# Layer 0's attention matrix as the stationary operand of the mixing product

## The reference

```python
energy = einsum('bnc,bcm->bnm', x_q, x_k)        # x_q = (w_qk y)^T, x_k = w_qk x
attention = softmax(energy, axis=-1)
attention = attention / (1e-07 + attention.sum(axis=1, keepdims=True))
x_r = einsum('bcn,bnm->bcm', x_v, attention)     # x_v = w_v x + b_v
x_r = relu(einsum('oc,bcn->bon', w_t, x - x_r) + b_t)
x1 = x + x_r
```

## Time and profile before

| | before |
|---|---|
| median of 3 runs | 177.25 us (177.08 to 178.58) |
| span of the profiled execution | 174.3 us |
| PE busy | 149.8 us, 86% |
| DVE busy | 113.1 us, 65% |
| ACT busy | 99.7 us, 57% |
| POOL busy | 88.6 us, 51% |
| the chain that ended last, PE's share | 58% |

### The profile page before, as it was taken

How to read it: one execution, slowest core, us unless ns; L and a number is a source line. 1 busy time by engine, 2 the same in 40 slices (tenths; PEclk the granted TensorE clock), 3 DMA queues, 4 the chain that set the end, 5 groups by cost and what they waited for, 6 DMA issues and landing times.

```text
span 174.3 us, 3459 instructions
## 1 busy us (share of the span) xinstructions
PE 149.8 (86%) x1228; PEld 115.7 (66%) x1228; DVE 113.1 (65%) x249; ACT 99.7 (57%) x242; POOL 88.6 (51%) x143
## 2 busy tenths in 40 slices
PE   7699999999968795779972983865999999999994
PEld 6475677787843372545852852653787999888993
DVE  1445444997885227898999999998476630377310
ACT  2017877779867856557566865955875525255000
POOL 8905608478988850686145695698542544000000
PEclk9999999999999999579997598798799999999999
DMA  2998320201201100000000000000000001000101
GB/s 73 308 223 276 63 64 0 64 0 60 66 11 50 60 0 0 4 2 0 4 2 0 4 4 0 0 4 0 0 0 4 0 30 64 30 0 2 34 30 60
DMA packets 6722, 6.94 MB, mean 40 GB/s; under 512 B 956, under 2 KB 6098, under 8 KB 6706
## 3 DMA queue, kind: packets, MB, share of 16 engines
q1 hardware_dynamic: 5808, 5.85, 10.4%
q0 software_dynamic: 224, 0.33, 1.8%
q10 hardware_dynamic: 674, 0.56, 1.0%
HBM read 5.68 MB, written 1.05 MB: 39 GB/s over the span
## 4 chain that ended last, share of the span: by engine, by line
PE 58%; DVE 15%; POOL 13%; issue 7%; ACT 3%; DMA 2%; POOLq 0%; DVEq 0%
PE psum L779 53%; DVE probs L732 3%; DVE smax L740 3%; POOL us L338 3%; DMA vec_rows<-in_L_xattn_b_t_dram 2%; DVE psums L615 2%; PE psum L1007 2%; DVE probs L747 2%; POOL wpj_lo L314 2%; POOL wfc_lo L314 1%; POOL hidT_lo L366 1%; POOL rstd L302 1%; POOL probs L375 1%; POOL rows L319 1%; DVE xn L631 1%
## 5 line engine op out<-in xcount | busy, mean ns | idle before, releaser
L338 POOL TENSOR_SCALAR us<-uext,rinv 128x128 f32<-128x128 f32 x32 | 12.4, 399 | 15.8 <-DVE rinv L594 15.2
L375 POOL TENSOR_TENSOR probs<-probs,pinv 128x512 f32<-128x512 f32 x16 | 16.5, 1055 | 7.0 <-DVE pinv L620 7.0
L779 PE MATMUL psum<-wpj_hi,ff_hi 128*128 128x256 f32 x64 | 18.3, 286 | 0.0
L779 PE MATMUL psum<-wpj_hi,ff_lo 128*128 128x256 f32 x64 | 17.9, 280 | 0.0
L779 PE MATMUL psum<-wpj_lo,ff_hi 128*128 128x256 f32 x64 | 17.9, 280 | 0.0
L392 ACT ACTIVATE ys<-psum,vec 128x512 f32<-128x512 f32 x16 | 11.0, 687 | 10.5 <-PE psum L779 10.3
L673 DVE TENSOR_REDUCE nmax<-psum 128x2 f32<-128x512 f32 x16 | 10.3, 685 | 9.4 <-PE psum L779 9.4
L779 PE MATMUL psum<-att,us 128*128 128x256 f32 x64 | 15.2, 381 | 0.7 <-POOL us L338 0.7
L779 PE MATMUL psum<-hidT_hi,wfc_hi 128*128 128x512 f32 x32 | 13.8, 432 | 2.0 <-POOL hidT_lo L366 2.0
L437 ACT ACTIVATE att<-psum,nmax 128x256 f32<-128x256 f32 x32 | 14.7, 471 | 0.3 <-DVE nmax L673 0.2
L534 ACT ACTIVATE probs<-probs 128x512 f32<-128x512 f32 x16 | 9.9, 629 | 8.7 <-DVE probs L747 8.4
(11 more groups left out here) (111 smaller groups left out, 396.8 us busy)
## 6 DMA issues: line engine op xcount, KB each, us to landing
wstage<-in_L_xattn_fc_w_dram SPq DMA_DIRECT2D x4, 256.0 KB, 5.8
wstage<-in_L_xattn_proj_w_dram SPq DMA_DIRECT2D x4, 256.0 KB, 2.7
out_dram<-rows SPq DMA_DIRECT2D x8, 128.0 KB, 1.7
ys<-in_ctx_dram SPq DMA_DIRECT2D x1, 512.0 KB, 6.1
rows<-in_x_dram SPq DMA_DIRECT2D x1, 512.0 KB, 8.4
ys<-in_ctx_dram ACTq DMA_DIRECT2D x1, 384.0 KB, 5.2
rows<-in_x_dram SPq DMA_DIRECT2D x1, 384.0 KB, 5.9
wk<-in_L_xattn_k_w_dram SPq DMA_DIRECT2D x1, 256.0 KB, 6.2
```

The costliest lines, as they stand in the source:

```text
L338: pool.tensor_scalar(us[:, n % 2, e, j, :], uext[:, n % 2, j, e * C:e * C + P], rinv[:, n % 2, e, j:j + 1], 1.0, ALU.mult, ALU.mult).then_ ...
L375: pool.tensor_tensor(half, half, pinv[:, n % 2, k].unsqueeze(2).broadcast_to([P, H // 2, C]), ALU.mult).then_inc(S["probs_ready"], 1)
L779: return pe.matmul(dst, lhsT, rhs, start=start, stop=stop)
```

## The change

- The mixing product is transposed: `att` is the stationary operand (128 columns of it at a time) and `us` moves, now only 65 columns: 64 of scaled u, and the inverse row sum, which makes the column sum. A pair takes 8 products instead of 4. The result has positions on partitions, and one column sum for each.
- u and w_t x come from one pass: stationary `rows` (64 x 128, one image), moving `wtvt` = [(w_t w_v)^T, w_t^T], 128 columns. Four products on 64 rows of the array in place of two on 128. The separate product `wtx` goes. Results of the two images lie in banks 3 and 4. DVE takes them out at once with both biases (`evict_uw`), into four buffers `uw`.
- All four results of a mixing lie in one bank, 5, for every pair; it is no longer doubled.
- DVE inverts the column sums (`colsum`, `csinv`, 128 x 4 each) and makes `rin` in four operations of 64 columns. PE turns `rin` back by two transposes (`turn_rin`), and one DVE operation takes relu and residual (`residual`). ACT's Ln, Exp and relu, DVE's `mix_normed` and POOL's residual go.
- ACT, not DVE, copies `gx` out, between the exponentials of image 0 and of image 1.
- b_v and b_t come by DMAs into the layout in which they are used; their transpose on PE goes.

The core of the diff:

```diff
+        PROJ0, ENERGY, UW, BACK, MIX, TURN, FILL = 0, 1, 3, 4, 5, 6, 7
         MLP_BANKS = [4, 5, 4, 5]
-        SETUP_WT, SETUP_GRAM, SETUP_WTV, SETUP_VEC0, SETUP_WTBV, SETUP_VEC = 6, 5, 3, 4, 4, 6
+        SETUP_WT, SETUP_GRAM, SETUP_WTV, SETUP_WTBV, SETUP_VEC = 6, 5, 3, 5, 6
...
+        uw_ps = psum[:, UW:UW + 2, D:2 * D].rearrange("p e (j b c) -> p e j b c", j=2, b=2)
+        mix_ps = psum[:, MIX, 0:4 * (C + 2)].rearrange("p (k c) -> p k c", k=4)
...
-            load_vec(pool, 0, "b_v", L0_BV, vec0_loaded)
-            load_vec(pool, 0, "b_t", L0_BT, vec0_loaded)
+            pool.dma_start(bv_col[:], A["L0_xattn_b_v"].rearrange("(c o) -> c o", o=1)).then_inc(bv_loaded, 16)
+            pool.dma_start(brow[:, 1, :], A["L0_xattn_b_t"].rearrange("(o c) -> o c", o=1)
+                           .broadcast_to([P, C])).then_inc(bt_loaded, 16)
...
-            def residual(n):
-
-                wait(pool, "relu_out", n + 1)
-                pool.tensor_tensor(rows[:, n, :], rows[:, n, :], rout[:], ALU.add).then_inc(S["x1_ready"], 1)
...
-                            pool.tensor_scalar(us[:, n % 2, e, j, :], uext[:, n % 2, j, e * C:e * C + P],
-                                               rinv[:, n % 2, e, j:j + 1], 1.0, ALU.mult,
+                            pool.tensor_scalar(us[:, n % 2, e, j, 0:C], uw[:, n % 4, e, j, 0, :],
+                                               us[:, n % 2, e, j, C:C + 1], 1.0, ALU.mult,
                                                ALU.mult).then_inc(S["scaled_u"], 1)
-                if 0 <= t - 2 < N - 1:
-                    residual(t - 2)
...
                         gelu(act, 0, u)
 
-            def relu(n):
-                wait(act, "relu_in", n + 1)
-                wait(act, "x1_ready", n)
-                if n == 0:
-                    act.wait_ge(vec0_ready, 1)
-                act.activation(rout[:], rin[:, n % 2, :], ACT.Relu, bias=col(L0_BT)).then_inc(S["relu_out"], 1)
+            def gx_copy(n):
+                wait(act, "gx_made", n + 1)
+                wait(act, "energy_made", 2 * (n - 1))
+                act.copy(gx[:, n % 2, :], halfbank(PROJ0, 0)).then_inc(S["gx_ready"], 1)
...
                 if 0 <= t < N:
                     energy_exp(t, 0)
+                if 0 <= t + 1 < N:
+                    gx_copy(t + 1)
                 if 0 <= t < N:
                     energy_exp(t, 1)
-                if 0 <= t - 2 < N - 1:
...
                     fill(u)
-                n = t - 1
-                if 0 <= n < N:
-
-                    wait(act, "mixed", 2 * n + 2)
-                    for e in range(2):
-                        act.activation(csln[e * C:(e + 1) * C, :],
-                                       psum[(1 - e) * C:(2 - e) * C, MIX + n % 2, e * D:(e + 1) * D], ACT.Ln,
-                                       bias=COLSUM_EPS).then_inc(S["colsum_ln"], 1)
-                    wait(act, "colsum_ln", 2 * n + 2)
-                    wait(act, "mix_normed", 2 * n)
...
-                if t == N:
-                    relu(N - 1)
...
             def rowsum_inv(n, e):
                 wait(dve, "energy_exp", 2 * (2 * n + e + 1))
-                wait(dve, "scaled_u", 4 * (n - 1))
-                dve.reciprocal(rinv[:, n % 2, e, :], rsum[:, n % 2, e, :]).then_inc(S["rowsum_inv"], 1)
-
-            def mix_normed(n):
-
+                wait(dve, "mixed", 2 * (n - 2) + e + 1)
+                dve.reciprocal(us[:, n % 2, e, :, C], rsum[:, n % 2, e, :]).then_inc(S["rowsum_inv"], 1)
+
+            def evict_uw(n):
+                wait(dve, "uw_made", n + 1)
+                if n == 0:
+                    dve.wait_ge(wtbv_made, 1)
+                    dve.tensor_copy(brow[:, 0, :], psum[:, SETUP_WTBV, 0:C]).then_inc(wtbv_ready, 1)
+                    dve.wait_ge(wtbv_ready, 1)
+                    dve.wait_ge(bt_loaded, 16)
+                dve.tensor_tensor(uw[:, n % 4].rearrange("p e j b c -> p e j (b c)"),
+                                  uw_ps.rearrange("p e j b c -> p e j (b c)"),
+                                  brow[:].rearrange("p b c -> p (b c)").unsqueeze(1).unsqueeze(1)
+                                  .broadcast_to([P, 2, 2, P]), ALU.add).then_inc(S["uw_ready"], 1)
+
+            def relu_in(n):
+
+                wait(dve, "mixed", 2 * n + 2)
+                dve.tensor_scalar(colsum[:], mix_ps[:, :, C], -1.0, -COLSUM_EPS, ALU.mult,
+                                  ALU.add).then_inc(S["colsum_eps"], 1)
+                wait(dve, "colsum_eps", n + 1)
+                dve.reciprocal(csinv[:], colsum[:]).then_inc(S["colsum_inv"], 1)
                 wait(dve, "colsum_inv", n + 1)
-                for e in range(2):
-                    dve.tensor_tensor(mixn[e * C:(e + 1) * C, :],
-                                      psum[e * C:(e + 1) * C, MIX + n % 2, e * D:(e + 1) * D],
-                                      csinv[e * C:(e + 1) * C, :], ALU.mult).then_inc(S["mix_normed"], 1)
-
-            def relu_in(n):
-
-                wait(dve, "mix_normed", 2 * n + 2)
-                wait(dve, "wtx_made", n + 1)
-                wait(dve, "relu_out", n - 1)
-                dve.tensor_tensor(rin[:, n % 2, :], halfbank(WTX, 0), mixn[:],
-                                  ALU.subtract).then_inc(S["relu_in"], 1)
+                wait(dve, "rin_turned", n - 1)
+                for i in range(2):
+                    for e in range(2):
+                        k = 2 * i + e
+                        dve.scalar_tensor_tensor(rin[:, n % 2, i, e * C:(e + 1) * C], mix_ps[:, k, 0:C],
+                                                 csinv[:, k:k + 1], uw[:, n % 4, e, i, 1, :], ALU.mult,
+                                                 ALU.add).then_inc(S["rin_ready"], 1)
+
+            def residual(n):
+                wait(dve, "rin_turned", n + 1)
+                dve.scalar_tensor_tensor(rows[:, n, :], halfbank(BACK, 0), 0.0, rows[:, n, :], ALU.max,
+                                         ALU.add).then_inc(S["x1_ready"], 1)
 
...
+                if 0 <= t - 3 < N - 2:
+                    residual(t - 3)
...
-                n = t + 1
-                if 0 <= n < N:
-                    wait(dve, "proj_made", n + 1)
-                    dve.tensor_copy(gx[:, n % 2, :], halfbank(PROJ0, 0)).then_inc(S["proj_ready"], 1)
-                    wait(dve, "scaled_u", 4 * (n - 1))
-                    if n == 0:
-                        dve.wait_ge(wtbv_made, 1)
-                        dve.tensor_copy(wtbv[:], psum[:, SETUP_WTBV, 0:P]).then_inc(wtbv_ready, 1)
-                        dve.wait_ge(wtbv_ready, 1)
-                        dve.wait_ge(zeros_ready, 3)
-                    dst = uext[:, n % 2, :, :].rearrange("p j (b c) -> p j b c", b=3)[:, :, 0:3:2, :]
-                    dve.tensor_tensor(dst, halfbank(PROJ0, 1).rearrange("p (j b c) -> p j b c", j=2, b=2),
-                                      wtbv[:].rearrange("p (b c) -> p b c", b=2).unsqueeze(1)
-                                      .broadcast_to([P, 2, 2, C]), ALU.add).then_inc(S["proj_ready"], 1)
+                if 0 <= t + 1 < N:
+                    evict_uw(t + 1)
...
-                if 0 <= t - 2 < N - 1:
-                    mix_normed(t - 2)
...
+                        residual(N - 2)
...
+                        residual(N - 1)
...
-            pe.wait_ge(vec0_loaded, 2 * 16)
-            pe.transpose(psum[:, SETUP_VEC0, 0:VEC_ROWS - L0_BV], vec0_rows[:],
-                         ident[0:VEC_ROWS - L0_BV, 0:VEC_ROWS - L0_BV]).then_inc(vec0_turned, 1)
...
-            def wtx(n):
-                wait(pe, "relu_in", n)
-                mm(halfbank(WTX, 0), wtT[:], rows[:, n, :]).then_inc(S["wtx_made"], 1)
+            def proj(n):
+                if n == 0:
+                    pe.wait_ge(gram_ready, 2)
+                landed(pe, x_loaded, n)
+                wait(pe, "gx_ready", n)
+                wait(pe, "uw_ready", n)
+                mm(halfbank(PROJ0, 0), gram[:], rows[:, n, :]).then_inc(S["gx_made"], 1)
+                if n == 0:
+                    pe.wait_ge(wtv_ready, 1)
+
+                wait(pe, "x1_ready", n - 3)
+                for j in range(2):
+                    for e in range(2):
+                        r = slice(e * C, (e + 1) * C)
+                        ins = mm(psum[:, UW + e, D + j * P:D + (j + 1) * P], rows[r, n, j * P:(j + 1) * P],
+                                 wtvt[r].rearrange("p b c -> p (b c)"))
+                ins.then_inc(S["uw_made"], 1)
+
+            def mix(n):
+                wait(pe, "rin_ready", 4 * n)
+                for e in range(2):
+                    wait(pe, "scaled_u", 2 * (2 * n + e + 1))
+                    for i in range(2):
+                        for j in range(2):
+                            ins = mm(mix_ps[:, 2 * i + e, 0:C + 1], att[:, n % 2, e, j, i * P:(i + 1) * P],
+                                     us[:, n % 2, e, j, 0:C + 1], j == 0, j == 1)
+                    ins.then_inc(S["mixed"], 1)
+
```

(36 more changed lines are left out.)

## The result

The changed kernel is slower: 202.49 us (median of 4 runs, 201.12 to 204.91) against 177.69 us for the kernel before, run beside it; the ratio is 1.146, 95% interval 1.136 to 1.156. The profiled execution spans 201.3 us against 174.3.

A forecast was written before the change was run, and what follows sets the result against it. The prediction took PE to set the pace with POOL close behind. Span 174.3 + 15.1 (loop) - 1.5 (end of layer 0) + 5 (clock) = 192.9 us; with 2.95 from span to median, 196, range 186 to 203.

The forecast's parts named there:

- the case that was forecast: Whole kernel: load-bound mixing on a closed loop, with some falls of the clock; 191 to 201 us, chance 0.55.
- rival 3: The clock falls in every step, or load and pass run in turn; 203 us, 201 to 210, chance 0.15.
- loop of steps 2 to 6, full clock: Steps 2 to 6: each lasts 8.1 to 8.3 us because the mixing waits behind the softmax; +15.1 us.
- mixing itself: PE's mixing product: 1.75 us after the change against 1.73 before, taken as the same.
- setup and steps 0, 1: Steps 0 and 1: PE's extra edits left against the setup's shorter chain; 0, within 1 us either way.
- end of layer 0, full clock: From step 7's energies to `probs`: -2.2 as `rin` needs no ACT, +0.7 for two residuals; net -1.5 us.
- clock: Steps 3 to 7: clock falls to half in several; 1.7 us in three of five steps, +5 us, bounds 0 and 10.
- The new wait: PE's mixing waits for DVE's `rin` of pair t-2 behind the second inverse, starting about 6.0 us after the energies.
- The load-bound mixing: 16 mixing passes, each priced by its full weight load at 0.11 us, not by its columns; 1.75 us.
- Rival 2: Short mixing passes stream at 0.055 us with hidden loads; 188 us, 184 to 191, chance 0.18.
- The relief of DVE, ACT and POOL: Work removed from these engines is worth nothing under an 8 us loop.
- Rival 5: The mixing's wait is met in time, so POOL's relief counts; 173 us, chance 0.03.

The follow-up runs named there:

- e3: The changed kernel with unused products of ones added on PE ahead of the mixing's wait in steps 2 to 7; 190.4 us, ratio 1.082.
- e4: The changed kernel with ten unused products added in each of steps 3 to 7, moving 32, 65, 96, 128 and 192 columns in turn; 192.34 us.
- e1: The changed kernel with DVE's `relu_in` of pair t-2 moved ahead of the row maxima of pair t; 178.70 us, ratio 1.009.
- e5: The changed kernel with the transfer spreading `b_t` over 128 partitions issued behind the memset of `vals`; 200.75 us, ratio 1.134.
- e12: A repeat of e7's kernel, unchanged; 171.09 us, ratio 0.969.
- e7: e1 with e5's later transfer, and the casts of steps 1 to 7 moved from DVE to the end of ACT's step; 173.05 us, ratio 0.979.

## Why the prediction was right or wrong, point by point

The mechanism was right and the size too small: 196 was said, 202.5 came, at the very edge of the range of 186 to 203 (1.146 times the 177.25 us that the prediction started from is 203.1). It lies outside the 191 to 201 of the case that was forecast and inside the 201 to 210 of rival 3, which had a chance of 0.15. In spans the miss is larger, 192.9 against 201.3: the 2.95 us that the prediction added from span to median, where 1.2 were measured, covered 1.8 us of it. The terms, at their own clock, in us of the profiled executions:

| term | said | measured | from |
|---|---|---|---|
| loop of steps 2 to 6, full clock | +15.1 | +13.1 | e3, 39.0 against 25.9 |
| mixing itself | 0 | 0 | e4; 2.00 against 1.89 |
| setup and steps 0, 1 | 0 | +2.1 | energies(2), 25.32 against 23.18 |
| end of layer 0, full clock | -1.5 | -2.5 | e3, 15.89 against 18.42 |
| behind the first `probs` | 0 | +0.6 | 107.4 against 106.8 |
| clock | +5 | +14 | changed kernel less e3, 201.3 against 187.3 |

(The clock row compares whole spans, so beside it stand e3's own setup, 1.9, and tail, 0.6: with them the column comes to 27. The loop and the end came out 3.0 us below what was said, the setup and the tail 2.7 above; that these cancel is luck, and what is left of the miss is the clock.)

- **The new wait: right**, in place, releaser and length: 6.0 us were said from the energies to the mixing, 5.5 measured. The last inverse came at 4.1, the two small operations took 0.3 (said 0.4), `rin` 0.87 with its waits (said 1.0), and the copy of `gx` only 0.26 of the chain (said 0.40). e1 shows that this wait is what holds the loop.
- **The load-bound mixing: right.** 16 passes are done in 1.90 to 2.00 us at the full clock, 0.11 apart, and e4 shows the price flat up to 128 columns. Rival 2, passes at 0.055, is out. The 0.11 also is what the Trainium skill gives for a load of 128 columns (TensorE: Matmul & The Clock Gate, LDWEIGHTS).
- **The clock: the term that was mis-sized.** The price of a fall in one step was well estimated: 3.4 us for the whole of PE's work on the loop, and steps 4 and 5 measured 3.0 each over e3. The step that failed is "I take half of that, 1.7, in three of the five steps, because a fall need not cover it all". That gave 5 us, with a bound of 10; 14 were measured. Falls covered all of it in steps 4 and 5, more than half in 3 and 6 (1.9 and 2.3 us), and step 7's stretch to `probs`, which the sum had left out, lost 3.5 more. The wait that let the clock fall comes back in every step, and the work that is released by it runs right behind it, so the low clock and the critical work coincide. That is rival 3's first half, which was given 203. By the ratios, 1.146 and 1.082, the fillers are worth 11 us; by the two profiles 14.
- **The setup: a term put at 0, wrong by 2.1 us.** "The setup's shorter chain" was set against PE's extra passes. The chain did lose the transpose of `b_t`; but `b_t` became a broadcast of 32 KB, which was not looked at as a DMA at all, and e5 shows that it makes the first loads late. Of the 2.1 us, 0.9 are the later start of energies(0), 0.9 a longer step 0, with PE's passes slow for longer, and 0.3 a longer step 1 (7.79 us against 7.45: from 15.73 to 23.18 before, from 17.53 to 25.32 after), with PE busy all through in both. More tiling changes and the turned uw are the likely reason for these 0.3; no run tests it.
- **The end of layer 0: right in sign**, and larger, -2.5, when the clock holds; the falls turned it into +0.9.
- **The relief of DVE, ACT and POOL: right** that it is worth nothing in the steps of the loop. Without the loop e12 gains 6.3 us at the end of layer 0. That is the whole change and not this relief alone: PE was idle 3.2 of the 18.42 us there and is idle 0.4 of 12.15 in e12, and its `wtx` products are gone too. Rival 5 had set 173 for a wait met in time, and named DVE's order as the point from which it decides; e1 is that edit. It gave 178.7, with a rest of DVE's lateness, a fall of the clock and the late loads in its trace; with the casts moved and the transfer late it came to 171 to 173.

## What to carry to other kernels

When two buffers become one, look for the operation that frees it and for what stands ahead of it in its engine's order, not for how long it takes: here four operations of 0.9 us together cost 13 us of loop and 11 to 14 of clock, and moving the call above the maxima gave nearly all of it back. Count a recurring wait of TensorE twice, once for itself and once for the work behind it at the lower clock, and cover in that second count every stretch in which it recurs. In float32 with stationary operands of 128 columns, as here, a moving operand of fewer than 128 columns makes no pass cheaper (e4): there the number of passes is what counts.

## What was not expected of the hardware

- A broadcast of a 64-element vector to 128 partitions, 32 KB, kept the DMA engines full while they moved 133 to 164 GB/s (four profiles) instead of 284 to 355 (nine). Small and spread was not cheap here.
- A DVE cast of 128 x 512 took 0.39 us in one step and 1.02 in the next, where POOL's subtraction of the low part (41.33 to 42.60 us in e1) ran beside it; `maskadd` took 0.41 and 0.94 in the same way. Not any work of POOL does it: the cast of 0.39 us ran at 36.46 while POOL scaled `us` (36.09 to 36.95). By what path the two engines meet no run here tells.
- Work added to a waiting engine made the kernel 12 us faster (e3). It is the lesser cure: the moved call is worth twice as much.
- Step 0's energies took 1.71 to 2.09 us in every profile (1.81 in the kernel before), where at the full clock they take 1.14 later. In the changed kernel the granted clock was 0.50 there; in the kernel before, in e3 and in e7 it read 1.00. Why the passes were slow under a full reading stays open.
